# A decoder kernel: softmax sums of 14 of 16 units a layer as rows through DRAM, heads scaled on GpSimd, both ends batch by batch

## What is computed

```
x = x + gelu(linear_attention(layernorm(x)))            # elu+1 features, 128 wide
y = layernorm(x)
for l in range(4):                                      # 8 heads of 64, rope on 32
    y = y + softmax(rope(q) rope(k)^T + mask) v  Wo     # 512 keys, 512 queries a batch
    y = y + softmax(rope(q) rope(kc)^T) vc  Wo          # 154 context keys
    y = y + gelu(rms(y) W1 + b1) W2
x = x + rms(y) * g_out
x = x + 8 experts, gates by top-p                       # 128 -> 512 -> 128
x = x + decayed causal linear attention
x = x + masked cross attention, 16 heads of 8
x = x + 8 gated experts, top 2, and a shared one        # 128 -> 384 -> 128
```

## Time and profile before

| | |
|---|---|
| median of 3 runs (lowest, highest) | 1288.48 us (1288.14, 1288.56) |
| the profiled execution | 1288.1 us, span 1286.4 us |
| PE busy, weight loads | 1137.9 us (88%), 752.9 us |
| DVE, ACT, POOL busy | 777.5, 704.1, 556.1 us |
| mean granted PE clock | 0.948 |
| chain that ended last | PE 72%, DVE 12%, POOL 6%, ACT 5%, DMA 4% |

### The profile page before, as it was taken

The page is one execution under the profiler, slowest core; times in us unless marked ns, Lnnn a source line. Parts: engine busy times, 40 slices in busy tenths (PEclk is TensorE's granted clock), DMA queues, the critical chain, the costliest instruction groups (busy, mean ns, idle before and its releaser), DMA issues.

```text
span 1286.4 us, 21103 instructions
## 1 busy us (share of the span) xinstructions
PE 1137.9 (88%) x7320; PEld 752.9 (59%) x7320; DVE 777.5 (60%) x2164; ACT 704.1 (55%) x1889; POOL 556.1 (43%) x643
## 2 busy tenths in 40 slices
PE   4389998989999998999999899999759995899698
PEld 2255655566566565556656656556549983454487
DVE  7776766567676647666565757756243125676466
ACT  2087665637676645777654776756234534365333
POOL 2366843457673437775345777434120100110211
PEclk8599999989999999999999999999869997899699
DMA  4001110001011000200100011100121100000011
GB/s 144 16 1 26 18 42 10 25 1 40 18 18 50 6 22 1 48 18 17 43 26 1 2 42 26 34 2 1 27 67 44 39 18 0 2 1 1 1 47 38
DMA packets 60280, 31.58 MB, mean 25 GB/s; under 512 B 34260, under 2 KB 51473, under 8 KB 60177
## 3 DMA queue, kind: packets, MB, share of 16 engines
q1 hardware_dynamic: 60177, 30.23, 9.0%
HBM read 29.06 MB, written 1.16 MB: 23 GB/s over the span
## 4 chain that ended last, share of the span: by engine, by line
PE 72%; DVE 12%; POOL 6%; ACT 5%; DMA 4%; issue 2%; SPq 0%; POOLq 0%; DVEq 0%
PE bank L1665 12%; PE bank L1642 7%; PE bank L1725 7%; PE bank L1619 7%; PE bank L1882 4%; PE bank L1693 3%; PE bank L1611 2%; PE bank L1813 2%; PE bank L1815 2%; PE bank L1814 2%; DMA dram_r<-recs 2%; PE bank L1676 2%; PE bank L1696 2%; PE bank L1694 2%; PE bank L1989 2%
## 5 line engine op out<-in xcount | busy, mean ns | idle before, releaser
L955 DVE CUSTOM_DVE_ANT_0 bank<-bank,maskrow 128x512 f32<-128x512 f32 x256 | 172.4, 715 | 83.1 <-PE bank L1619 82.4
L1363 ACT ACTIVATE probs<-bank,tops 128x512 f32<-128x512 f32 x256 | 174.7, 689 | 86.0 <-DVE tops L955 85.5
L1375 ACT ACTIVATE KA<-bank 128x512 f32<-128x512 f32 x256 | 139.2, 602 | 22.7 <-PE bank L1642 20.8
L1619 PE MATMUL bank<-QR 64*128 64x512 f32 x768 | 126.9, 437 | 13.4 <-DVE QR L1008 12.4
L1642 PE MATMUL bank<-ident,probs 128*128 128x128 f32 x1024 | 134.5, 274 | 1.6 <-ACT KA L1375 1.4
L1642 PEld LDWEIGHTS bank<-ident,probs 128*128 128x128 f32 x1024 | 116.8, 141 | 31.5 <-issue 10.9
L1665 PE MATMUL bank<-KA,Vs 128*64 128x512 f32 x512 | 127.5, 608 | 0.0
L1359 ACT ACTIVATE probs<-bank,tops 128x154 f32<-128x154 f32 x256 | 96.3, 388 | 44.0 <-DVE tops L952 43.5
L943 DVE TENSOR_TENSOR rot<-bank,cos 128x512 f32<-128x512 f32 (+1 forms) x112 | 73.3, 655 | 52.2 <-PE bank L1696 41.1
L1619 PEld LDWEIGHTS bank<-QR 64*128 64x128 f32 x768 | 64.8, 190 | 42.7 <-issue 34.3
L978 DVE TENSOR_TENSOR AT<-bank,recT 128x512 f32<-128x512 f32 x64 | 43.4, 678 | 71.9 <-ACT recT L1380 41.8
(11 more groups left out here) (280 smaller groups left out, 2508.1 us busy)
## 6 DMA issues: line engine op xcount, KB each, us to landing
recT<-dram_r SPq DMA_DIRECT2D x56, 128.0 KB, 3.3
W<-in_W SPq DMA_DIRECT2D x8, 256.0 KB, 3.0
Vc<-in_wup SPq DMA_DIRECT2D x8, 224.0 KB, 2.5
W<-in_sWk SPq DMA_DIRECT2D x4, 256.0 KB, 4.2
W<-in_sWq SPq DMA_DIRECT2D x4, 256.0 KB, 4.5
W<-in_sWv SPq DMA_DIRECT2D x4, 256.0 KB, 4.9
wo<-in_sWo SPq DMA_DIRECT2D x4, 256.0 KB, 2.7
ck<-in_cWk SPq DMA_DIRECT2D x4, 256.0 KB, 2.8
```

Source lines behind the costliest of these rows:

```text
L955: v.tensor_tensor_reduce(bank[i][:, :], bank[i][:, :], maskrow[:, u.b * S:(u.b + 1) * S], -SCALE, 3.0e38, ALU.add, ALU.min, tops[:, g % 4, ...
L1363: c.activation(to, bank[i][:, :], ACT.Exp, bias=tops[:, g % 4, e, 0:1], scale=-1.0, accum_out=sums[:, n, e, k:k + 1]).then_inc(q.probs_rea ...
L1375: c.activation(turned_self(u)[:, half, :, k * P:(k + 1) * P], bank[4 + half][:, :].rearrange("p (c t) -> p c t", t=P), ACT.Copy).then_inc( ...
L1619: ins = mm(bank[first + e][:, :], QH[rows_of(e), u.j, a, w], KH[rows_of(e), u.j, c, :], start=(n == 0), stop=(n == 2))
```

## The change

`NEAR` shrinks to units 7 and 15. For the other 14 PE transposes the sums themselves (`turn_sums`, 128 x 8 to 8 x 128) into bank 5, DVE takes the reciprocals there (8 partitions x 128), SP writes them as eight rows of 512 bytes and reads them back broadcast. DVE copies bank 6 to the heads unscaled, and POOL multiplies them by recT in place (`scale_heads`, at the steps `SCALED`); sout and cout wait for that too, and a slot of recT is written again only after it. The two near units copy their spread into the heads' place and DVE multiplies there. All tables have other entries. Before the layers, ACT takes the positive part, the values and the adding of one from DVE, with the sum of the keys, and the second root is worked out from the first one and the variance. Behind the first experts each norm, turn and projection is done for one batch as soon as it is there, the last attention's keys and values and some constants move behind expert 3, ACT's extra pass before the logarithm becomes its bias, and the gate logic of the last experts comes after both batches' gates. The upper triangle is made after the layers, in the cosine table's place.

```diff
 SELF = (
-    "k0.2", "q0.2", "turn1", "k0.3",
-    "v1.0", "", "k1.0", "q0.3",
-    "v1.1", "k1.1", "q1.0", "",
-    "v1.2", "v1.3", "", "q1.1",
-    "q1.2", "k1.2", "k1.3", "q1.3",
-    "", "sout0", "norm0 ck.1", "turn0",
-    "cq0.0", "cq0.1", "", "ck.2",
-    "", "ck.3", "cq0.2", "cq0.3",
+    "q0.2", "turn1", "k0.2", "k0.3",
+    "q0.3", "v1.0", "k1.0", "",
+    "q1.0", "k1.1", "q1.1", "v1.2",
+    "", "k1.2", "v1.3", "v1.1",
+    "q1.2", "", "", "sout0",
+    "k1.3", "norm0", "q1.3", "ck.1",
+    "", "turn0", "cq0.0", "",
+    "cq0.2", "cq0.1", "ck.3", "cq0.3",
 )
 CROSS = (
-    "", "sout1", "", "cv.2 norm1",
-    "turn1", "cq1.0", "cv.3 cq1.1", "cq1.2",
-    "", "cq1.3", "", "cout0 norm0",
-    "", "", "turn0", "",
+    "ck.2", "sout1", "cv.2", "norm1",
+    "turn1", "cq1.0", "cq1.1", "cv.3",
+    "cq1.2", "cq1.3", "", "cout0 norm0",
+    "", "turn0", "", "",
 )
-BEFORE = ("+turn0@7 +k0.0@6 +q0.0@5 +k0.1@4 +q0.1@7 +v0.0@6 +v0.1@5 first0.0 first0.1 +v0.2@4 +v0.3@7 +cv.0@6 "
-          "+cv.1@5 +ck.0@7")
-END = ("up0@0123 out spread pv.0 pv.1 down0@0 norm0 cout1@3 norm1 +cv.1@0 +ck.0@5 +cv.0@7 +turn0@2 +v0.1@3 "
-          "+v0.0@4 +k0.0@3 +q0.0@7 turn1@4 +k0.1@0 +q0.1@3 up1@4567 first0.0 first0.1 down1@6 +v0.3@4 +v0.2@7 "
-          "norm1")
+BEFORE = ("+turn0@7 +k0.0@0 +q0.0@5 +k0.1@4 +v0.0@0 +v0.1@5 +q0.1@3 first0.0 +v0.3@7 first0.1 +v0.2@4 +cv.0@6 "
+          "+cv.1@3 +ck.0@7")
+END = ("out up0@0123 spread pv.0 pv.1 down0@3 norm0 cout1@4 norm1 +turn0@2 +ck.0@4 +cv.0@3 +k0.0@3 +cv.1@0 "
+          "+q0.0@2 turn1@4 +k0.1@5 +v0.0@2 +v0.1@0 +q0.1@0 up1@4567 first0.0 first0.1 down1@6 +v0.2@3 norm1 "
+          "+v0.3@6")
 WEIGH = {
-    0: (4, 6, 6, 7),
-    1: (9, 9, 11, 11),
-    2: (13, 13, 13, 15),
-    3: (17, 17, 18, 19),
-    4: (20, 22, 22, 23),
-    5: (24, 25, 27, 27),
-    6: (28, 29, 29, 31),
+    0: (5, 7, 7, 7),
+    1: (8, 9, 11, 11),
+    2: (14, 14, 14, 14),
+    3: (18, 18, 18, 18),
+    4: (20, 21, 21, 23),
+    5: (24, 26, 27, 27),
+    6: (28, 29, 29, 29),
     7: (32, 32, 32, 32),
     8: (34, 35),
-    9: (36, 37),
-    10: (38, 38),
-    11: (40, 41),
-    12: (42, 42),
+    9: (37, 38),
+    10: (39, 39),
+    11: (41, 41),
+    12: (43, 43),
     13: (44, 45),
-    14: (47, 47),
+    14: (46, 46),
 }
-LATE = (14, 17, 26, 34, 38, 39, 40, 42, 44, )
+LATE = (7, 8, 17, 27, 34, 38, 42, )
 SPREAD = {u: at[-2] for u, at in WEIGH.items()}
 DONE = {u: at[-1] for u, at in WEIGH.items()}
-NEAR = (7, 8, 9, 10, 11, 12, 13, 14, 15, )
+SCALED = {u: 4 * u + 6 for u in range(8)}
+SCALED.update({8 + c: min(36 + 2 * c, 47) for c in range(7)})
...
+NEAR = (7, 15, )
...
+    return rows_sent(n) % 2
...
-                sp.dma_start(dram_r[i].rearrange("e t p -> p (e t)"), recs[:, i, :, :].rearrange("p e t -> p (e t)"),
-                             allow_slow_non_contiguous=True).then_inc(q.rec_out, 16)
+                sp.dma_start(dram_r[i].rearrange("e t p -> (e t) p"), recrow[:, rows_sent(u.n) % 2, :]).then_inc(q.rec_out, 16)
                 sp.wait_ge(q.rec_out, 16 * rows_sent(u.n))
-                if u.n >= 2:
-                    sp.wait_ge(q.heads_ready, u.n - 1)
+                if rows_sent(u.n) > 2:
+                    sp.wait_ge(q.heads_scaled, rows_sent(u.n) - 2)
                 for e in range(2):
-                    sp.dma_start(recT[e * DH:e * DH + DH, u.n % 2, :],
-                                 dram_r[i, e].rearrange("t p -> (t p)").partition_broadcast(DH)).then_inc(q.spread_in, 16)
+                    sp.dma_start(recT[e * DH:e * DH + DH, slot(u.n), :],
+                                 dram_r[i, e].rearrange("t p -> (t p)").partition_broadcast(DH)).then_inc(
+                                     (q.spread_in0, q.spread_in1)[slot(u.n)], 16)
...
+            def scale_heads(u):
+                pool.wait_ge(q.heads_ready, u.n + 1)
+                pool.wait_ge((q.spread_in0, q.spread_in1)[slot(u.n)], 32 * ((rows_sent(u.n) + 1) // 2))
+                o = AT[:, u.j, u.b * S:(u.b + 1) * S]
+                g.tensor_tensor(o, o, recT[:, slot(u.n), :], ALU.mult).then_inc(q.heads_scaled, 1)
...
+                    for u in step.scale:
+                        scale_heads(u)
...
+            def linear_minimum(b):
+                for k in range(2):
+                    dve.wait_ge(q.lin_full, 3 * b + k + 1)
+                    v.tensor_scalar(elu[b][:, k, 0, :], bank[3 * b + k][:, :], cols[:, k:k + 1], 0.0, ALU.add,
+                                    ALU.min).then_inc(q.lin_min, 1)
+            def linear_parts(b):
+                for k in range(2):
+                    dve.wait_ge(q.lin_max, 2 * b + k + 1)
+                    dve.wait_ge(q.lin_exp, 2 * b + k + 1)
+                    v.scalar_tensor_tensor(out=elu[b][:, k, 1, :], in0=elu[b][:, k, 0, :], scalar=-1.0, in1=elu[b][:, k, 1, :],
+                                           op0=ALU.add, op1=ALU.add).then_inc(q.lin_part, 1)
+            def linear_attention(b):
+                w = slice(b * S, (b + 1) * S)
+                dve.wait_ge(q.lin_add, 2 * b + 2)
+                link(v.tensor_scalar(z0T[:, w], q0T[:, w], kv[:, 2 * b + 1:2 * b + 2], 1.0e-6, ALU.mult, ALU.add))
+                v.reciprocal(z0T[:, w], z0T[:, w])
+                dve.wait_ge(q.lin_value, b + 1)
+                link(v.tensor_tensor_reduce(o0T[:, w], k0T[:, w], v0T[:, w], 1.0, 0.0, ALU.mult, ALU.add, kv[:, 2 * b:2 * b + 1]))
+                v.scalar_tensor_tensor(out=o0T[:, w], in0=q0T[:, w], scalar=kv[:, 2 * b:2 * b + 1], in1=z0T[:, w],
+                                       op0=ALU.mult, op1=ALU.mult).then_inc(q.lin_ready, 1)
+            def linear_out(b):
+                dve.wait_ge(q.gelu_ready, see.next(q.gelu_ready))
+                w = slice(b * TB, (b + 1) * TB)
+                return v.tensor_tensor(x[:, w, :], x[:, w, :],
+                                       g0[:, b * S:(b + 1) * S].rearrange("p (t d) -> p t d", d=D), ALU.add)
+            def second_root(b):
+                w = slice(b * TB, (b + 1) * TB)
+                dve.wait_ge(q.rstd_ready, see.next(q.rstd_ready))
+                link(v.tensor_tensor(square[:, w], rstd[:, w], rstd[:, w], ALU.mult))
+                link(v.tensor_tensor(square[:, w], square[:, w], mv[:, w, 1], ALU.mult))
+                v.tensor_scalar(square[:, w], square[:, w], 1.0e-16, None, ALU.max).then_inc(q.var_ready, 1)
+            def centred_by(dst, by, b):
+                for t in range(b * TB, (b + 1) * TB):
+                    ins = v.tensor_scalar(dst[:, t, :], x[:, t, :], mv[:, t, 0:1], by[:, t:t + 1], ALU.subtract, ALU.mult)
+                ins.then_inc(q.normed, 1)
+            def two_norms():
+                link(linear_out(0))
+                norm_stats(0, x, False)
+                linear_out(1).then_inc(q.x_final, 1)
+                second_root(0)
+                dve.wait_ge(q.x_final, 1)
+                norm_stats(1, x, False)
+                for b in range(B):
+                    if b:
+                        second_root(b)
                     w = slice(b * TB, (b + 1) * TB)
-                    ins = v.tensor_tensor(x[:, w, :], x[:, w, :],
-                                          g0[:, b * S:(b + 1) * S].rearrange("p (t d) -> p t d", d=D), ALU.add)
-                    if b == 0:
-                        link(ins)
-                ins.then_inc(q.x_final, 1)
-                dve.wait_ge(q.x_final, 1)
+                    dve.wait_ge(q.rstd_ready, see.next(q.rstd_ready))
+                    link(v.tensor_tensor(root[:, w], root[:, w], rstd[:, w], ALU.mult))
+                    centred_by(nx, root, b)
+                for b in range(B):
+                    centred_by(y, rstd, b)
+                see.expect(q.normed, 6)
+                dve.wait_ge(q.normed, see.now(q.normed))
...
-                dve.wait_ge(q.probs_ready, 2 * step.g + 2)
                 n = step.unit.n
-                v.reciprocal(recs[:, n % 4, :, :], sums[:, n % 4, :, :]).then_inc(q.rec_ready, 1)
+                if n % (2 * UNITS) in NEAR:
+                    dve.wait_ge(q.probs_ready, 2 * step.g + 2)
+                    v.reciprocal(recs[:, n % 4, :, :], sums[:, n % 4, :, :]).then_inc(q.rec_ready, 1)
+                else:
+                    dve.wait_ge(q.sums_full, rows_sent(n))
+                    if rows_sent(n) > 2:
+                        dve.wait_ge(q.rec_out, 16 * (rows_sent(n) - 2))
+                    v.reciprocal(recrow[:, rows_sent(n) % 2, :], bank[5][0:2 * TB, 0:P]).then_inc(q.rec_ready, 1)
             def normalise(u):
+                o = AT[:, u.j, u.b * S:(u.b + 1) * S]
                 if u.n % (2 * UNITS) in NEAR:
                     dve.wait_ge(q.spread_ready, u.n + 1 - rows_sent(u.n))
+                    dve.wait_ge(q.weighed, u.n + 1)
+                    v.tensor_tensor(o, bank[6][:, :], o, ALU.mult).then_inc(q.heads_ready, 1)
                 else:
-                    dve.wait_ge(q.spread_in, 32 * rows_sent(u.n))
-                dve.wait_ge(q.weighed, u.n + 1)
```

(98 more changed lines are left out.)

333 lines of the change are left out of this document (180 added, 153 removed).

## The result

The changed kernel takes 1271.93 us (median of four runs, 1269.68 to 1274.52), the kernel before beside it 1288.52. The ratio is 0.986, its 95% interval 0.982 to 0.990: faster by 16.6 us or 1.4%, where 48 us were forecast, and outside the range of 1216 to 1262. All ratios here leave out three executions that took over 1.5% longer than the fastest of their kernel (1435.2 us in e2, 1339.1 in e5, 1274.1 in e12). The profiled execution took 1271.0 us, span 1269.3.

A forecast was written before the change was run, and what follows sets the result against it. PE was taken to bound layers and experts, chains through DVE, ACT and POOL both ends. Layers 20 (5.05 x 4), start 7.4, decay and last attention 14.1, last experts 6.8: 48.3 off 1288.5 gives 1240 us, range 1216 to 1262.

The forecast's parts named there:

- PE's work, 5.3: Layers: seven spreads leave PE (6.8 us), 14 lone transposes come (1.5 us); net 5.3 us less PE work a layer.
- END, + 1.0: Layer end: first keys and queries ahead of the values start POOL's ropes sooner, shortening PE's 2.6 us wait; 1 us a layer.
- The wait for bank 5, - 2.1: Layers: bank 5 is held until DVE's long reciprocal ends, so PE stands 0.15 us a unit; 2.1 us lost a layer.
- POOL, - 1.5: Layers: 14 new POOL multiplies of 1.28 us delay ropes, cross tails, sout and cout; 1.5 us lost a layer.
- Bank 7, + 1.6: Cross attention: two PE waits of 0.8 us for ACT to empty bank 7 go with the spreads; 1.6 us a layer.
- the first unit's DMA, + 0.75: A layer's first unit: the wait through the 10.7 us write of sums moves off DVE; 0.75 us a layer on average.
- Rival B: Layers give nothing: PE's 5.3 us become waits for bank 5, the long reciprocal and POOL's queue; 1260 us, chance 0.15.
- The start: Before the layers: shorter DVE chain, low part of the input at 47.75 against 55.13 us; 7.4 us, bounds 5 and 9.
- Decay and last attention: After the first experts: queries(0) 18.1 us earlier, less 2.0 in the experts and 2.0 in the attention; 14.1 us.
- The last experts: Gated experts: second expert at 1217.3 against 1224.06 us, later ones keeping their pace, PE bound; 6.8 us, bounds 4 and 8.
- The write: Layers: SP's new write of a unit's sums, eight rows of 512 bytes, taken as 2.4 us; sum holds below 6 us.
- Rival D: Layers: the write still takes 8.55 us, so POOL, tails and PE stand behind it; 69 us lost, 1309 us, chance 0.03.

The follow-up runs named there:

- e2: Changed kernel with DVE taking short reciprocals of the 128 x 8 sums first and ACT copying the turned row: 1263.2 us, ratio 0.981.
- e5: Changed kernel with the step tables of the kernel before, sums still sent as rows and GpSimd still scaling: 1318.7 us, ratio 1.022.
- e12: Layers of the kernel before with the changed ends, PE's filler transposes, and gated-expert products right behind each batch's adding: 1258.1 us, ratio 0.980 to before.
- e7: Changed kernel plus 58 unread PE transposes of the identity in its waits of the decay stage: 1266.5 us, ratio 0.984.
- e9: Changed kernel with the tables BEFORE and END of the kernel before, all else unchanged: 1269.9 us.
- e3: Changed kernel with DVE's 8 x 128 reciprocal replaced by a copy of the row, output not the reference's: 1269.0 us.
- e4: Changed kernel with each GpSimd multiply of the heads cut from 512 columns to 16, output not the reference's: 1272.5 us.
- e13: Changed kernel with BEFORE and END of before, a copy for the long reciprocal and GpSimd's multiply cut to 16 columns: 1251.1 us, ratio 0.971.
- e1: Layers of the kernel before with the changed kernel's start, decay stage, last attention and gated experts: 1262.6 us, ratio 0.982.
- e8: Changed kernel plus unread PE transposes in the waits of the decay stage, the start and ahead of the first experts: 1263.3 us, ratio 0.980.

## Why the prediction was wrong

**The step that failed** is the sum a layer: + 5.05 forecast, - 2 measured (5.9 over three periods). Of the 31.7 us between 48.3 and 16.6, the layers make some 26 (20 forecast, about - 6 measured) and the ends some 5 (28.3 forecast, 23 measured). Term by term:

- PE's work, 5.3: right in kind. Measured 4.1, and 4.5 between periods with no time at the lower clock (201.8 in e12, 197.3 in e7). The two prices nearly held: a spread's 16 records add 0.88 us to PE's busy time in the three periods (0.97 forecast), a lone transpose 0.09 (0.11; its record is 0.27 us long, but those of its neighbours overlap it). That makes 4.9; where the rest went isn't shown.
- END, + 1.0: wrong in sign, - 1.7 (e9). I priced the wait that the new order removes and not the turn that it brings forward onto a norm that isn't ready.
- The wait for bank 5, - 2.1: too much, 0.9 a layer (0.07 x 14) at `turn_sums` and 0.4 at the half-turns. It was looked for on PE. The cost came by DVE, at whose queue the reciprocal and the wait for PE's transpose take 1.6 us a unit. "It lies beside PE" was the error: with 0.67 us less of each reciprocal, PE idles 1.8 us a layer less (e3).
- POOL, - 1.5: 0.3 (e4). POOL's multiplies of 1.28 us really lie beside PE.
- Bank 7, + 1.6, and the first unit's DMA, + 0.75: the waits for ACT's copy of recT are gone, all but the 0.8 a layer of the near unit 7 (now before L1827), and so are those for the 10 us write. But other waits took their place: END and a layer's first steps, self attention and cross attention idle 1.2, 2.1 and 2.7 us more, not less, and 1.5 of the last stays when the three causes are out (e13). Nothing in the sum asked, for each wait that went, which one is next there; only for the small, added costs was that done.

Rival B named this mechanism (PE's 5.3 us become waits for the long reciprocal and other queues) and put it at no gain, 1260, at 0.15. In the layers it was B and 6 us more; the other 6 us or so between 1260 and 1271.9 are the ends. Its "for" was right and its "against" (DVE and POOL under 75%) was the usual trap: a busy share says nothing of the order in a queue.

**The start** (7.4): right, a little better. The second batch's long reciprocal starts at 27.32 and not at 33.63, PE turns at 40.64, and the low part, which I set at 47.75, starts at 46.59 against 55.13: 8.5. The first END gains 7.6, or 8.7 with the layer of before (e1); that lies near the upper bound of 9.

**Decay and last attention** (14.1): the chain was right, 17.6 against 18.1, the first scores 43.8 us behind the last product of the experts. Keys and values in the experts cost 1.4 (forecast 2.0). The attention's term of 2.0 is the one that was mis-sized: 1.4 of work, a little less than forecast, and 5.2 of clock. In the kernel before, the half clock of 1104.1 to 1111.0 us, behind the wait in this line, fell on the turn and the queries, and the first scores began at full clock:

```profile
1105.97 2.14 PE L1573 MATMUL bank<-ident,nx 128*128 128x128 f32 x8 [4.08 <-DVE nx L879]
```

In the kernel after it lasts from 1093.4 to 1107.0, over the scores. That the shorter stage is what moved it there is read from the traces; e8 shows that it stays away when the waits are filled.

**The last experts** (6.8): 4.9. The second expert did come 9.2 us sooner after the attention's last scores, more than the forecast. But then: "the experts after it keep their pace" failed. The gate logic and the adding behind it stand behind the first products now, on DVE from 1200.99 to 1208.97, and the second expert's products wait for it:

```profile
1209.79 3.47 PE L2290 MATMUL bank<-cv,probs 128*128 128x128 f32 x16 [2.66 <-DVE probs L1371]
```

Of the 9.2 us 4.2 were given back; that wait and the clock of 0.87 from 1203 to 1216 us stand where it happened: a wait was moved, not removed.

**The write** (2.4 us): behind its issue SP waited 0.87 us on average for it to land (45.4 us over 52 times), 1.8 at most, where it had waited 9.0 on average before (251.2 us over 28 times). Rival D's premise is gone. The Trainium skill's rule in "DMA: Bandwidth & Descriptors" (Specifications) on pieces from 512 B up agrees with this trace, which can't tell it from the fall in their number from 1024 to 8. The other page of the Trainium skill that was weighed, "SBUF — State Buffer" (Who interferes with whom), would have given up to 20 us against the change; DVE's low halves, with two SBUF inputs, took 889 ns in the median against 893, so none of it came: none of the 16 overlaps a scaling. The rule itself does show in this trace: the eight low halves that overlap one of POOL's rope multiplies took 1.09 to 1.53 us, the other eight 0.68 to 0.69.

**The marks.** A layer near 213 us failed (217 to 219). "PE idle over 0.5 us a unit at turn_sums", a sign of being wrong, did not come (0.07): the 6.1 us of added idle time a layer stand elsewhere, so the marks would not have led to the cause. And 0.2% was too fine for what a measurement can tell: the interval of the ratio is 0.8% wide.
